# A perceiver layer with a mixture of experts: the end of its attention part ordered by hand

## The reference

```
x = x + cross_attention(norm(x), context)      # one head, width 512, biases bq, bk, bv
x = x + self_attention(norm(x))                # 16 heads of 32, masked; queries from
                                               # a normalised 128-wide compression, keys and values from another
x = x + moe(norm(x))                           # 16 experts, 4 per token, inner width 256,
                                               # squared relu, sigmoid router in 4 groups;
                                               # plus a shared expert of inner width 1024
```

## Time and profile before

| | us |
|---|---|
| median of 3 runs | 368.29 (366.7 to 370.63) |
| the profiled execution | 368.43 |
| its span in the trace | 366.7 |
| TensorE busy | 341.3 |
| VectorE busy | 245.0 |
| ScalarE busy | 189.8 |
| GpSimd busy | 86.9 |

### The profile page before, as it was taken

One profiled execution on the slowest core, in us unless ns is written; L12 is line 12 of the kernel. 1 busy time (PEld: TensorE's weight loads), 2 busy tenths in 40 slices (PEclk: granted clock), 3 DMA queues, 4 the chain that ended last, 5 costly groups with the idle time before them and its releaser, 6 DMA issues.

```text
span 366.7 us, 6992 instructions
## 1 busy us (share of the span) xinstructions
PE 341.3 (93%) x2530; PEld 238.7 (65%) x2530; DVE 245.0 (67%) x479; ACT 189.8 (52%) x428; POOL 86.9 (24%) x106
## 2 busy tenths in 40 slices
PE   6999799999999989987799789999998999999996
PEld 5987567677677767766587768888643444444344
DVE  2875978746588377566775665991534776778587
ACT  2457574635566574464564661412134677777520
POOL 3600500000012011411413404004336544432000
PEclk9999999999999999998958899999999999999999
DMA  6982689976222355074000156589934453331573
GB/s 234 405 349 107 231 333 418 387 238 227 88 86 87 109 166 215 29 279 181 29 2 2 35 177 249 229 301 413 389 109 158 156 173 125 126 101 59 200 288 114
DMA packets 17185, 69.70 MB, mean 190 GB/s; under 512 B 2816, under 2 KB 3328, under 8 KB 14592
## 3 DMA queue, kind: packets, MB, share of 16 engines
q1 hardware_dynamic: 12768, 56.93, 40.8%
q0 software_dynamic: 3520, 11.54, 8.9%
q10 hardware_dynamic: 864, 0.79, 0.7%
HBM read 61.91 MB, written 7.34 MB: 189 GB/s over the span
## 4 chain that ended last, share of the span: by engine, by line
PE 70%; DVE 15%; ACT 6%; issue 4%; DMA 2%; POOL 1%; another core or an unknown queue 1%; ACTq 0%; DVEq 0%
PE bank L1828 10%; PE bank L1796 9%; PE bank L1404 8%; PE bank L1669 8%; PE bank L1406 8%; PE bank L1405 8%; PE bank L1765 2%; ACT hw L843 2%; DMA raw<-in_wkT 2%; PE bank L1555 2%; PE bank L1839 2%; PE bank L1807 2%; DVE stats L957 2%; DVE cT L1163 2%; PE bank L1639 2%
## 5 line engine op out<-in xcount | busy, mean ns | idle before, releaser
L1669 PE MATMUL bank<-ring,wT 128*128 128x384 f32 x128 | 44.0, 487 | 0.7 <-ACT wT L799 0.7
L1796 PE MATMUL bank<-WX,xsT 128*32 128x256 f32 (+1 forms) x256 | 38.0, 380 | 0.9 <-ACT hs L877 0.9
L1828 PE MATMUL bank<-WX,hsT 128*32 128x512 f32 (+1 forms) x128 | 38.2, 598 | 0.0
L1163 DVE TENSOR_TENSOR cT<-ring_T,cT 128x512 fp32r<-128x512 f32 x45 | 31.0, 732 | 6.5 <-ACT cT L705 6.5
L1669 PEld LDWEIGHTS bank<-ring,wT 128*128 128x128 f32 x128 | 23.6, 190 | 14.2 <-ACT wT L799 0.9
L1796 PEld LDWEIGHTS bank<-WX,xsT 128*32 128x32 f32 x256 | 17.8, 110 | 21.9 <-issue 11.8
L1336 DVE COPY down_copy<-WX 128x1024 f32 x32 | 21.0, 697 | 14.9 <-PE bank L1828 14.9
L1796 PE MATMUL bank<-up_copy,xsT 128*32 128x256 f32 x384 | 30.7, 379 | 0.0
L1828 PE MATMUL bank<-down_copy,hsT 128*32 128x512 f32 x192 | 30.7, 598 | 0.0
L705 ACT CAST cT<-ring_T 128x512 fp32r<-128x512 f32 x48 | 27.0, 618 | 6.5 <-PE bank L1406 6.3
L843 ACT ACTIVATE hw<-bank,hnb 128x128 f32<-128x128 f32 x64 | 22.7, 371 | 13.5 <-DVE hnb L986 13.5
(11 more groups left out here) (289 smaller groups left out, 877.2 us busy)
## 6 DMA issues: line engine op xcount, KB each, us to landing
WX<-in_experts SPq DMA_DIRECT2D x16, 1024.0 KB, 6.9
ring_T<-in_ctxT SPq DMA_DIRECT2D x16, 768.0 KB, 7.2
ring<-in_ctx SPq DMA_DIRECT2D x16, 768.0 KB, 5.1
WX<-y_rows SPq DMA_DIRECT2D x4, 1024.0 KB, 8.1
raw<-in_experts SPq DMA_DIRECT2D x3, 1024.0 KB, 4.9
raw<-in_wqT SPq DMA_DIRECT2D x4, 256.0 KB, 5.8
res<-in_x SPq DMA_DIRECT2D x4, 256.0 KB, 8.4
raw<-in_woT SPq DMA_DIRECT2D x1, 1024.0 KB, 5.6
```

The costliest lines, as they stand in the source:

```text
L1163: V_.tensor_tensor(cT[:, g % 2, 1, t, :], ring_T[:, g % RING_T, t, :], f32(cT[:, g % 2, 0, t, :]), ALU.subtract).then_inc(cTlo_ok, 1)
L1669: last = mm(bank[B_O][:, 0:TD], wT[:, g % 2, k * P:(k + 1) * P], ring[:, g % RING, k, :], start=(c == 0 and k == 0), stop=(c == NCH - 1 an ...
L1796: last = mm(bank[B_H[g % 2]][q * SLOT:(q + 1) * SLOT, 0:IC * P], xsT[:, g % 2, c * P + q * SLOT:c * P + (q + 1) * SLOT], w, start=c == 0, ...
L1828: last = mm(bank[B_Y[g % 2]][q * SLOT:(q + 1) * SLOT, :], hsT[:, g % 2, m * P + q * SLOT:m * P + (q + 1) * SLOT], w, start=m == 0, stop=m ...
```

## The change

The list of steps ends with step 20 (`TAIL` = 21). What stood in steps 21 to 33 becomes functions, called one by one in an order written out for each engine. Beside the order:

- From unit 8 on the scores use three banks (6, 4 and 0), and a pair waits for one unit's exponentials fewer.
- From unit 8 on the exponentials use four buffers (`hw_more`, in the place of routed expert 4) and wait for the transposes three units back. Expert 4 is loaded behind the last unit's transposes.
- The low parts of shared blocks 0 and 1 are made by GpSimd, in eight halves, early; their high parts by ScalarE at the start of the stretch.
- Batch 2's output projection goes to bank 1, and bank 1 also serves the rows of batches 0 to 2.
- The places of `u_w` and `d_w`, and with them the order of some loads, are exchanged.

```diff
-        u_w = [at(f"u_w{e}", [P, 2, HALF], wx_place((12, 6, 3, 13)[e]), F32R) for e in range(NSH)]
-        d_w = [at(f"d_w{e}", [P, 2, HALF], wx_place((8, 15, 14)[e]), F32R) for e in range(NSH - 1)]
+        u_w = [at(f"u_w{e}", [P, 2, HALF], wx_place((6, 3, 12, 13)[e]), F32R) for e in range(NSH)]
+        d_w = [at(f"d_w{e}", [P, 2, HALF], wx_place((8, 14, 15)[e]), F32R) for e in range(NSH - 1)]
+        hw_more = at("hw_more", [P, 4, HT * P], wx_place(4))
+        def hw_of(u):
+            return hw[:, u % 2, :] if u < 2 * ROWS else hw_more[:, u % 4, :]
...
+            return 1 if b < NB - 1 else B_S
+        def wo_bank(b):
+            return 1 if b == NB - 2 else B_S
...
-            return 0 if u % 2 else 6
+            return (6, B_O, 0)[u % 3 - 2] if u >= 2 * ROWS else 0 if u % 2 else 6
...
             sp.wait_ge(o_mm, G)
-            for e in (0, 1, 2, 4):
+            for e in (0, 1, 2):
                 load_routed(e)
             for e in range(FIRST):
-                sp.wait_ge(u_lo, e + 1)
-                sp.wait_ge(d_lo, e + 1)
+                sp.wait_ge(ulo_first, 2 * e + 2)
+                sp.wait_ge(dlo_first, 2 * e + 2)
                 load_expert(e + FIRST)
+            sp.wait_ge(hwT_mm, UNITS)
+            load_routed(4)
...
-            for step in range(1, STEPS):
+            for step in range(1, TAIL):
...
+            def half_low(part, e, h, hi_ok, lo_ok):
+                pool.wait_ge(hi_ok, e + 1)
+                o = (h + 2 * (part is d_part)) * HALF // 2
+                c = slice(h * HALF // 2, (h + 1) * HALF // 2)
+                nc.gpsimd.tensor_tensor(part(e, 1)[:, c], raw[:, e % 2, o:o + HALF // 2], f32(part(e, 0)[:, c]),
+                                        ALU.subtract).then_inc(lo_ok, 1)
...
+            unit_weights(7)
+            for h in range(2):
+                half_low(u_part, 0, h, u_hi, ulo_first)
+            inverse_root(norm_no["middle", 3])
+            half_low(u_part, 1, 0, u_hi, ulo_first)
+            unit_weights(8)
+            half_low(u_part, 1, 1, u_hi, ulo_first)
+            inverse_root_2(3)
+            unit_weights(9)
+            half_low(d_part, 0, 0, d_hi, dlo_first)
+            unit_weights(10)
+            last_rows(1)
+            half_low(d_part, 0, 1, d_hi, dlo_first)
+            unit_weights(11)
+            half_low(d_part, 1, 0, d_hi, dlo_first)
+            unit_weights(12)
+            half_low(d_part, 1, 1, d_hi, dlo_first)
+            for u in range(13, 16):
+                unit_weights(u)
+            last_rows(2)
+            last_rows(3)
...
+            def unit_exp(u):
+                b, r = divmod(u, ROWS)
+                act_e.wait_ge(hnb_ok, u + 1)
+                if 2 <= u < 2 * ROWS:
+                    act_e.wait_ge(hwT_mm, u - 1)
+                elif u >= 3 * ROWS:
+                    act_e.wait_ge(hwT_mm, u - 3)
...
+            sums_hi(3)
+            up_hi(0)
+            up_hi(1)
+            unit_exp(8)
+            unit_copy(6)
+            router_exp(0)
+            unit_copy(7)
+            rows_hi(norm_no["middle", 3], 3, bank[B_POST])
+            unit_exp(9)
+            attended_hi(1)
+            act_e.wait_ge(att_mm, NB)
+            down_hi(0)
+            act_e.wait_ge(down_mm, NB)
+            down_hi(1)
+            unit_exp(10)
+            compressed(3)
+            head_features(3)
...
+            attended_hi(3)
+            squared_half(0, 0)
+            rows_hi(norm_no["last", 2], 2, bank[rows_bank(2)])
+            router_exp(2)
+            relu_half(1, 0)
+            squared_half(1, 0)
+            for e in range(FIRST, NSH):
+                up_hi(e)
+                if e < NSH - 1:
+                    down_hi(e)
+            rows_hi(norm_no["last", 3], 3, bank[rows_bank(3)])
+            router_exp(3)
...
+            sums_lo(3)
+            inverse_sums(7)
+            mask_and_max(8)
+            cross_added(3)
+            find_masked(9)
+            normalise(m3, 3)
+            put_lowest(9)
+            highest(9)
+            inverse_sums(8)
+            rows_lo(m3, 3, bank[B_POST])
+            find_masked(10)
+            put_lowest(10)
+            attended_lo(1)
+            moments_2(3)
+            highest(10)
+            normalise_2(3)
+            inverse_sums(9)
+            find_masked(11)
+            self_added(1)
+            put_lowest(11)
+            highest(11)
+            moments(l1, 1)
+            inverse_sums(10)
+            normalise(l1, 1)
+            mask_and_max(12)
...
+            gated_half(1, 0)
+            normalise(l3, 3)
+            up_lo(FIRST)
+            rows_lo(l3, 3, bank[rows_bank(3)])
+            down_lo(FIRST)
...
+                if u > 2 * ROWS:
+                    pe.wait_ge(exp_ok, u - 1)
+                elif u >= 2:
                     pe.wait_ge(exp_ok, u)
...
+            sums_T(3)
+            pair_scores(8)
+            attended(3)
+            unit_T(6)
+            router(0)
+            unit_T(7)
+            rows_T(norm_no["middle", 3], bank[B_POST])
+            pair_scores(10)
+            unit_sums(1)
+            compress(3)
+            project(1)
+            compressed_T(3)
+            keys_and_queries(3, TAIL)
+            unit_T(8)
+            pair_scores(12)
+            unit_T(9)
+            values(3)
+            unit_T(10)
+            pe.wait_ge(rexp_ok, 1)
+            rows_T(norm_no["last", 1], bank[rows_bank(1)])
+            pair_scores(14)
+            unit_T(11)
+            router(1)
+            unit_sums(2)
+            unit_T(12)
+            for m in range(IC):
+                first_up(0, m)
+            unit_T(13)
+            project(2)
+            unit_T(14)
+            unit_T(15)
+            unit_sums(3)
+            rows_T(norm_no["last", 2], bank[rows_bank(2)])
+            for m in range(IC):
+                first_up(1, m)
+            project(3)
+            router(2)
+            first_down(0, 1)
+            first_down(0, 0)
+            rows_T(norm_no["last", 3], bank[rows_bank(3)])
+            first_down(1, 1)
+            router(3)
+            first_down(1, 0)
```

More of the change, by code:

```diff
@@ new lines, in values_copy, with router_exp @@
+            def values_copy(b):
+                act_e.wait_ge(qkv_mm, 3 * b + 3)
+                copy(v_s[:, b % 2, :], bank[B_S][:]).then_inc(qkv_ok, 1)
+            def router_exp(b):
+                act_e.wait_ge(lg_mm, b + 1)
+                nc.scalar.activation(r_exp[:, b, :], bank[rows_bank(b)][:, 0:NE], ACT.Exp, scale=-1.0).then_inc(rexp_ok, 1)
+            for step in range(1, TAIL):
+                if (b := batch_at(step, WO_STEP)) is not None:
+                    attended_hi(b)
@@ L1228, in _ @@
                         mask_and_max(u)
-                if (u := unit_at(step, 1)) is not None and step > G + 1 and u < UNITS - 1:
+                if (u := unit_at(step, 1)) is not None and step > G + 1:
                     inverse_sums(u)
@@ new lines, in compressed_T, with keys_and_queries @@
+            def compressed_T(b):
+                pe.wait_ge(cqn_ok, b + 1)
+                for i in range(2):
+                    last = nc.tensor.transpose(bank[B_POST][:, i * P:(i + 1) * P], cqn[:, i * P:(i + 1) * P], ident[:])
+                last.then_inc(cqT_mm, 1)
+            def keys_and_queries(b, step):
+                pe.wait_ge(cf_ok, b + 1)
+                pe.wait_ge(wu_in, 16)
+                for i in (1, 0):
+                    if i == 0 and step <= G:
+                        pe.wait_ge(s_ok, step - (step - 1) % 2)
+                    elif i == 0:
+                        pe.wait_ge(x2_ok, b - 1)
+                    for j in range(HT):
+                        last = mm(bank[(B_S, B_POST)[i]][:, j * P:(j + 1) * P], wu_s[:, i * D + j * P:i * D + (j + 1) * P],
+                                  cf[:, i, :], start=True, stop=True)
+                    last.then_inc(qkv_mm, 1)
@@ new lines, in values, with unit_sums @@
+            def values(b):
+                pe.wait_ge(qkv_ok, 3 * b + 2)
+                mm(bank[B_S][:], cf[:, 1, :], wu_s[:, 2 * D:3 * D], start=True, stop=True).then_inc(qkv_mm, 1)
+            def unit_sums(b):
+                pe.wait_ge(hwT_ok, ROWS * b + ROWS)
+                pe.wait_ge(qkv_ok, 3 * b + 3)
+                if b >= 1:
+                    pe.wait_ge(alo_ok, b)
+                for j in range(HT):
+                    for r in range(ROWS):
+                        h = j * ROWS + r
+                        last = mm(bank[B_A][r * DH:(r + 1) * DH, j * P:(j + 1) * P], v_s[:, b % 2, h * DH:(h + 1) * DH],
+                                  hwT(b * ROWS + r)[:, j * P:(j + 1) * P], start=True, stop=True)
+                last.then_inc(a_mm, 1)
@@ L1568, in chunk_T, with router @@
+            def router(b):
+                pe.wait_ge(xlo_ok, norm_no["last", b] + 1)
+                for c in range(DC):
```

(13 more changed lines are left out.)

415 lines of the change are left out of this document (215 added, 200 removed).

## The result

The changed kernel takes 366.37 us at the median of 20 runs (364.17 to 369.26), the kernel before 369.29 (366.7 to 372.51, 20 runs): a ratio of 0.9938, interval 0.9911 to 0.9965. It is faster by 0.6%, 2 or 3 us, where 8.6 were forecast. The profiled execution took 367.77 for a span of 366.0, the profiled one of before 368.43 for 366.7; both are within 1.5 of their medians.

The account below looks back on a forecast made before the run. It took TensorE, given weights, to bound everything behind shared block 2's start, and idle gaps and slow clock to cost time ahead. 11.6 saved, less 2.0 for clock and 1.0 for collisions, is 8.6: 359.8 us, range 355.5 to 365.5.

Parts of the forecast that it names:

- What bounds the kernel: TensorE bounds everything behind shared block 2's first matmul (230.87), so each microsecond by which that starts earlier reaches the end.
- The banks, buffers and order: From the sums' transposes to block 2: fewer waits, TensorE gaps 8.7 against 16.4, block 2 at 219.3, 11.6 us saved.
- the ledger: Hand-kept timing of the four in-order engine queues from 159.37 on; it reproduced the old order to 0.4 us.
- The price of nothing for expert 4's late load: Load moved to 195.6, first used past 250, DMA engines at 1% from 184 to 196: costed at nothing.
- The clock: Slow TensorE clock behind the one large gap left, before pair 14, costs 2.0 us, range 0 to 4.7.
- rival by the clock: Small gaps keep TensorE at 1.2 GHz before block 2: 378.6 us, each slow microsecond costing about 0.33; chance 0.05.
- The range: Run time 355.5 to 365.5 us, from the forecast's own costs, the GpSimd case and part of the last rival.
- Collisions: GpSimd and VectorE delay each other before block 2, as when normalising batch 3: 1.0 us, range 0 to 5.6.
- that rival: GpSimd is the bound: slow halves and products hold up units 9 to 13, 3.9 us left, 364.5; chance 0.14.
- Behind the stretch: From block 2's first matmul to the end TensorE's order is unchanged, so the 8.6 us pass on whole.
- the unknown wait: At 279.95 the chain stands 2.5 us behind something unknown; moved in time, it may vanish or grow.
- the ledger comes whole: No slow clock that counts and no collision before block 2: 11.6 us saved, 356.9; chance 0.17.

Follow-up runs that it names:

- the one at the full clock: Changed kernel with 13 added unread 512-column matmuls, five before batch 3's row transposes and eight before pair 14's scores: 359.09 us, ratio 0.9742 to the kernel before.
- the collision gone as well: Changed kernel with one GpSimd half moved behind unit 8's product and unread matmuls in two TensorE gaps (three and eight): 357.39 us, ratio 0.9731 to the kernel before.
- the first control: Changed kernel with 13 unread 512-column matmuls behind two TensorE gaps (five and eight) instead of in them: 362.73 us, ratio 0.9869 to the kernel before.
- the changed kernel with fillers: Changed kernel with 13 unread 512-column matmuls in two TensorE gaps, before batch 3's row transposes (five) and pair 14's scores (eight): 359.09 us, ratio 0.9742.

## Why the prediction was wrong

**What bounds the kernel: right.** Everything gained ahead of block 2 reached the end, to within the 1 to 3 us by which the distance behind it differs from kernel to kernel (135.4 to 138.8 in the profiles).

**The banks, buffers and order: right.** Gaps of 8.7 in the ledger, 8.1 in the trace after and 8.5 in the one at the full clock. The new order from landmark to landmark: 59.9 in the ledger, 61.4 measured at the full clock, 60.6 with the collision gone as well. The price of nothing for expert 4's late load held: its load is issued at 203.7, the first routed rows are multiplied at 259.1, and TensorE is busy for 32.00 of the 32 us from 230 on. Pair 12 and projection 3 came late (180.6 and 208.7 for 177.6 and 201 to 204), by slow clock: at the full clock they stand at 178.1 and 201.5.

**The clock: this step failed.** "I take 2.0, nearer the shorter pieces." It cost 9.2 (70.65 - 61.44), outside its own range of 0 to 4.7. Two things were wrong in it. I counted gaps ("the new order has one such gap") and the price of one slow piece; there were three slow pieces, 7.1, 11.1 and 3.5 us, and the first control shows that the work behind a gap decides too. The count was already loose in the kernel before, where the slow piece from 205.1 stands not only behind the gap of 1.43 but directly behind one of 1.22 that the prediction passed over, and begins within 256-column matmuls:

```profile
204.62 0.36 PE L1404 MATMUL bank<-xT_l,u_w 128*128 128x256 f32 x1 [1.22 <-issue]
```

```profile
205.00:208.75 3.75, 3.75 (x21) 3.75 (x21) 1.08 (x3) 3.04 (x11) 1.36 (x2) 0.54 0.00 0
```

And I carried over how little slow clock had cost. The ledger of the old order lost 4.2 to 17 slow us, 0.25 each, because its waits absorbed part of them: its gaps at the full clock come to 16.4 in the ledger, and the trace, with slow clock, has 11.1. The ledger is the only evidence for that, since the old order was never run at the full clock. The new order took the waits out (8.7 in the ledger, 8.1 in the slow trace: next to nothing absorbed), TensorE is itself the chain for long stretches, and 20 slow us (0.14 / 0.5 x 70.65) cost 9.2, 0.46 each. The prediction had a like number (0.33 each) in its rival by the clock, but not in its forecast: 20 us by it are 6.6.

**The range.** It does not follow from its parts either. Their lower bounds together give 354.4 and their upper ones 369.7 (356.9, and to it 4.7, 5.6 and 2.5); the prediction stated 355.5 to 365.5 without saying how the parts were joined.

**Collisions: right in size and place,** 1.0 taken for one or two hits, with "normalising batch 3 at 166 beside a half" named; 0.83 measured on that normalising, 0.86 at the end of the stretch. Its rows, though, were of subtractions with two SBUF operands, and the normalising has one such tile. By the Trainium skill, page "SBUF — State Buffer", section "SBUF: two separate sides", the pair of ports is also taken by VectorE operations in a mode that uses both ports, and the one that starts later waits for the whole of the other. Waiting for GpSimd's end (166.08) and then taking 0.55 would be 1.64; the trace has 1.38, so the wait here was shorter than that, and no run shows whether this normalising is in such a mode. GpSimd's halves took 1.25 to 1.28, near the 1.2. So that rival falls.

**Behind the stretch: "I pass the 8.6 on whole"** lost 1.3. Two things are new there: a slow piece of the clock behind the entries' narrow matmuls, which the prediction did not look for, and the unknown wait, 3.10 + 0.56 for 2.50, of which the prediction says that it may grow. Which of them costs the 1.3 stays open: the trace with the low parts on VectorE has the longer wait (3.35 + 0.55) and a distance of 135.4, and the one with only the second gap filled has neither in its chain and 138.7.

**The sum by its steps.** Forecast span 358.1. To it 7.2 for the clock (9.2 - 2.0), 0.5 for what the ledger had too short (61.4 - 59.9 - 1.0), 1.3 behind, less 1.1 for a stretch that began at 158.25 and not 159.37: 366.0, the span measured. It begins earlier since pair 8's scores, 1.09 us, have moved from ahead of the landmark to behind it; the prediction does not say whether its ledger from 159.37 on holds them; without them it would be too short by about that much. The rival "the ledger comes whole" (356.9) has no collision and no slow clock; the changed kernel with fillers took 356.8 in its one run at the full clock, collision included, so that the two agree to 0.1 is in part luck.

## What to carry to other kernels

Before taking waits out of a kernel, ask what they hid: slow clock that falls into a wait costs little, and on a path where the engine itself is the chain it cost 0.46 us for each slow one here. List the places where a gap of over half a microsecond is followed by narrow matmuls; there the granted clock is the thing to forecast, and wide work, one's own by a change of order or even unread, put into the gap paid here (ratio 0.9938 to 0.9731 for 11 added matmuls and one moved subtraction). Try both places, in the gap and behind it, and look at the trace: behind the first gap it held the clock, behind the second it did not. Test it in the kernel as it is after the change: the same remedy in the kernel before gave nothing, and there it did not hold the clock either.

## What the runs showed of the hardware

The granted clock of TensorE fell to 0.5 although the engine was busy for all of the piece (7.10 of 7.10 us): busy time is no sign of a full clock. It fell behind gaps of 1.51 and of 0.67 us followed by transposes and 32-row scores, not behind one of 1.50 where five 512-column matmuls followed the transposes, and behind one of 2.23 although five such matmuls followed at once. It also fell within wide matmuls (at 205.1 in the kernel before, at 221.2 in the changed one), and with no gap at all, behind the entries' 32 matmuls of 40 columns, in six of fifteen traces. At pair 14, with three score banks, it came back after 4 us in the three traces where wide matmuls (256 columns or more) stood early in the slow piece, after 10.5 to 11 in four where they came late, but after 7.5 and 4 in two more where they came late: early wide work goes with short slow pieces, and what ends one is not shown. The same kernel draws different clocks from run to run (0.966 to 0.976 here, 0.975 to 1.00 with fillers), and with them its time. A normalising with one large operand from SBUF took 1.38 instead of 0.55 beside a GpSimd subtraction.
